# Decoding 4-bit weights by column halves, and projecting the scan's input at the end of the first stage

## The chip, the cores and the metric

The kernel runs on one core of a Trainium2 chip. The metric is device time in microseconds (us) of that core for one execution, and a kernel's time is the median of its runs.

## The reference

Four layers of a gated model, each x = x + tanh(g) * attention-like part, then x = x + tanh(g) * feed-forward part, on x of 4 x 256 x 256 (T = 1024 rows of D = 256). The change touches the code of three of these parts: the first attention, the first feed-forward part (its weights are 4-bit codes with a scale for every 32 inputs) and the state-space scan of the fourth layer, whose input is the context and not x, so that the kernel computes it beside the first feed-forward part.

```python
# layer 0, feed-forward: 4-bit weights
idx = jnp.stack([W_packed & 15, W_packed >> 4 & 15], -1).reshape(N, -1)
W = (NVFP4_LUT[idx].reshape(N, K // 32, 32) * scales[:, :, None]).reshape(N, K)   # gate, up: 2048x256; down: 256x2048
# then down(gelu(gate(x)) * up(x)) on the normalized x

# layer 3, scan (hidden_states = context, 4x256x128)
x = jnp.einsum('bld,ed->bel', hidden_states, in_proj_w)      # the scan's side projection, 256 channels
x = silu(conv(x, conv_w, 4 taps) + conv_b)
dt_low, Bm, Cm = jnp.split(jnp.einsum('bdl,ed->bel', x, x_proj_w), [8, 24], axis=1)
dt = softplus(jnp.einsum('brl,dr->bdl', dt_low, dt_proj_w) + dt_proj_b)
# 256 steps: state = state * exp(dt * A) + dt * u * B ; y = sum(state * C)
```

## The kernel before

The kernel is a row of eight stages, `stage0` to `stage7`. Each is a block in which SyncE (SP, which issues most DMAs), TensorE (PE), VectorE (DVE), ScalarE (ACT) and GpSimd (POOL) run their own instruction lists, tied by semaphores; the next block begins when all five have ended. Memory is three large regions (regA, regB, regC) cut by hand, and some tiles of their own.

`stage0` is the first attention. SP loads x, projections, context and constants, and then the packed weights of the next stage: `load_packed` (line 205) issues for gate, up and down one DMA of codes (1 MB) and eight of scales (128 KB each, one row of scales spread over 16 partitions, line 207). PE projects the context to queries and keys (line 281), makes the energies (286), turns h and the attention matrix (185) and makes the mixing product (299). ACT takes the exponentials. DVE normalizes x (168), takes four maxima (311), divides, copies the turned attention, adds the result to x (330), and in between decodes weights: `dequant_on_vector` (216, 218, 226) is two tensor_scalars and one scalar_tensor_tensor over 128x2048, each waiting for the one before. A weight matrix takes two such steps (`par` 0 and 1). Four run in `stage0`: gate 0 after the maxima, gate 1 after the copies, up 0 and up 1 at the very end.

`stage1` holds the first feed-forward part and most of the scan. It first loads six constants of the scan (417). PE waits for them, projects the context in two halves of channels into the same pair of PSUM banks (`project_context`, 506), the second after ACT has copied the first to `xpad` (452), and turns h (185). DVE normalizes x, then convolves (`convolve`, 588 and 591); ACT takes Silu (458), PE makes `project_bc` (514). Then comes a loop over 32 units u: column chunk u mod 16 of the 2048 hidden columns, for one half of the rows. In each unit PE runs `gate_up(u+1)` (542) and `down(u)` (555), ACT the gelu (465), DVE the gated product `gated(u+1)` (674), and DVE has one more job: the two steps of the down weights in units 0 and 1, splitting rows in 2 and 3, nothing in unit 4, `softplus` in units 5 to 8 (620, 626, 631, 632, with ACT's squares, 447, between), and from unit 9 on one scan group for most units (654, 659, 667), which needs a row that PE spreads over the partitions (498). `down` of the first two units waits for its weights.

ACT takes units in pairs: gelu(0), gelu(1), then other work such as exponentials, then gelu(2), gelu(3). Each change of function set costs it a table load. DVE takes all in the order written.

## Time and profile before

| | us |
|---|---|
| runs (three) | 868.91, 872.73, 874.93 |
| median | 872.73 |
| the profiled execution | 877.0 |
| its span, first to last instruction | 875.2 |
| stage 0, from the start of the span | 0 to 48.9 |
| stage 1 | 48.9 to 267 |
| stages 2 to 7 | 267 to 875.2 |

The profiled execution is a single one and 0.5% above the median. Times in rows are from the start of its span. A row of the timeline is one instruction or several alike in a row (x4: four records); one PE matmul of 32-bit numbers shows as two records. "Idle before" is how long the engine had nothing to run, and what ended that. The granted clock is 1.00 for TensorE's full 2.4 GHz and 0.50 for 1.2 GHz. A DMA's time to landing counts from its issue on SP.

### The profile page before, as it was taken

The page shows a single profiled execution, that of the slowest core. Times are in us where ns is not written, and L with a number is a line of the kernel's source. Part 1 is how long each engine was busy: PE and PEld are TensorE (multiplying, and loading weights), DVE is VectorE, ACT ScalarE, POOL GpSimd, SP SyncE. Part 2 cuts the span into 40 slices and gives each one's busy share as a digit, 9 for nine tenths or more (in the row PEclk, how much of TensorE's full clock was granted, in tenths as well). Part 3 has the DMA queues.
Part 4 walks back from the last instruction along what each step waited for, and adds up shares of the span by engine and source line. Part 5 has one row for each costly group of instructions (what it writes and reads, how often), then busy time and mean ns, then how long its engine had stood idle before and what let it go on. Part 6 is the DMA issues. An engine that isn't in the chain of part 4 may idle for free. (4 is left out here: it accounts for less than half of the span.)

```text
span 875.2 us, 9489 instructions
## 1 busy us (share of the span) xinstructions
PE 649.1 (74%) x2849; PEld 403.9 (46%) x2849; DVE 647.2 (74%) x1331; ACT 355.6 (41%) x607; POOL 179.2 (20%) x184
## 2 busy tenths in 40 slices
PE   4549979999994547499928798889881687338991
PEld 3324545545553436367816455455450133235650
DVE  5988568997978887796546879889848988652344
ACT  5023476545421522455325455665622444402220
POOL 0000001211210000377261010110110255006651
PEclk9759999999996865699969779999986555558996
DMA  8500002454458406146420123433632500102225
GB/s 243 126 14 0 7 0 49 82 86 70 80 91 222 134 0 214 42 125 137 103 83 0 49 70 76 97 74 70 140 54 47 141 25 1 44 5 84 91 79 169
DMA packets 58151, 70.56 MB, mean 81 GB/s; under 512 B 16043, under 2 KB 41523, under 8 KB 56950
## 3 DMA queue, kind: packets, MB, share of 16 engines
q1 hardware_dynamic: 44934, 40.97, 16.7%
q0 software_dynamic: 13168, 28.97, 16.3%
q8 instruction: 25, 0.41, 0.2%
q14 instruction: 24, 0.20, 0.1%
HBM read 42.79 MB, written 10.36 MB: 61 GB/s over the span
## 5 line engine op out<-in xcount | busy, mean ns | idle before, releaser
L542 PE MATMUL ps<-hT,regA 128*128 128x512 f32 x256 | 116.7, 599 | 0.8 <-ACT hT L455 0.8
L1964 PE MATMUL ps<-regA,regD 128*34 128x256 f32 x256 | 71.5, 404 | 12.5 <-DVE h L2090 9.6
L542 PEld LDWEIGHTS ps<-hT,regA 128*128 128x128 f32 x256 | 48.9, 192 | 53.3 <-issue 48.9
L555 PE MATMUL ps<-regA,regC 128*128 128x256 f32 x256 | 64.5, 397 | 9.8 <-DVE regC L674 7.2
L555 PEld LDWEIGHTS ps<-regA,regC 128*128 128x128 f32 x256 | 47.7, 194 | 35.3 <-DVE regC L674 22.0
L719 POOL DMA_DIRECT2D yssm<-regB x19 | 23.0, 1212 | 185.2 <-DVE regB L667 185.2
L465 ACT ACTIVATE regC<-ps 128x512 f32<-128x512 f32 x32 | 19.0, 597 | 84.1 <-PE ps L542 83.9
L1811 ACT ACTIVATE regA<-ps 128x512 f32<-128x512 f32 x64 | 38.1, 596 | 31.6 <-PE ps L1950 31.0
L2070 DVE TENSOR_REDUCE regC<-ps 128x4 f32<-128x960 f32 x64 | 40.1, 685 | 9.6 <-PE ps L1914 9.6
L659 DVE TENSOR_TENSOR_SCAN regB<-regB 128x512 f32<-128x512 f32 x38 | 44.5, 1213 | 2.8
L1764 POOL DMA_DIRECT2D yssm<-regC x13 | 15.6, 1202 | 135.7 <-DVE regC L2111 119.1
L1309 POOL DMA_INDIRECT regA<-h_rows,regA x31 | 33.1, 1067 | 40.2 <-DVE regA L1586 31.1
L1964 PEld LDWEIGHTS ps<-regA,regD 128*34 128x34 f32 x256 | 24.3, 115 | 36.6 <-issue 10.3
L674 DVE TENSOR_TENSOR regC<-regC,ps 128x512 f32<-128x512 f32 x32 | 21.9, 683 | 24.1 <-ACT regC L465 23.6
L1622 DVE TENSOR_TENSOR regB<-regB,ps 128x176 f32<-128x176 f32 x23 | 7.8, 338 | 39.8 <-ACT regB L1368 39.8
L185 PE MATMUL ps<-ident,h 128*128 128x128 f32 x112 | 20.6, 353 | 22.3 <-DVE h L168 20.8
L173 ACT ACT_TABLE_LOAD x7 | 9.0, 1283 | 63.6 <-PEq L245 26.8
L1445 PE MATMUL ps<-regB,regA 128*128 x124 | 33.9, 397 | 0.0
L1903 PE MATMUL ps<-ident,regA 128*128 128x128 f32 x192 | 28.4, 311 | 6.5 <-DVE regA L2061 3.6
L1309 POOL DMA_INDIRECT regB<-h_rows,regB x23 | 22.5, 979 | 49.1 <-DVE regB L1581 42.4
L1445 PE MATMUL ps<-regA,regB 128*128 x92 | 32.2, 474 | 0.0
L2223 POOL TENSOR_TENSOR regB<-regB 128x1024 f32<-128x1024 f32 x8 | 21.7, 2710 | 47.4 <-DVE regB L2382 47.4
(419 smaller groups left out, 1572.8 us busy)
## 6 DMA issues: line engine op xcount, KB each, us to landing
yssm<-regB POOLq DMA_DIRECT2D x19, 512.0 KB, 5.0
regC<-bc_rows SPq DMA_DIRECT2D x26, 256.0 KB, 3.8
yssm<-regC POOLq DMA_DIRECT2D x13, 512.0 KB, 6.8
regB<-in_L_w SPq DMA_DIRECT2D x4, 1088.0 KB, 11.8
y_rows<-regA SPq DMA_DIRECT2D x31, 128.0 KB, 2.6
regB<-in_L_w SPq DMA_DIRECT2D x1, 2176.0 KB, 13.0
regC<-in_L_W SPq DMA_DIRECT2D x2, 1024.0 KB, 10.5
h_rows<-h SPq DMA_DIRECT2D x4, 512.0 KB, 6.7
```

What stands on the lines that cost most here:

```text
L542: m = nc.tensor.matmul(ps[:, 2 + 2 * (u % 2) + j, :], w[:, k * 2048 + c * P:k * 2048 + (c + 1) * P], hT[:, k, hf * HALF:(hf + 1) * HALF], ...
L555: m = nc.tensor.matmul(ps[:, t // 2, (t % 2) * D:(t % 2 + 1) * D], itm[:, u % 2, t * P:(t + 1) * P], WDv[:, c // 2, c % 2, :], start=(c == ...
L659: v.mark(nc.vector.tensor_tensor_scan(hs[:, k, :], dA[:, g % RD, k].rearrange("p b l -> p (b l)"), dBu[:, k, :], 0.0, ALU.mult, ALU.add))
L674: nc.vector.tensor_tensor(itm[:, u % 2, :], gel[:, u % 2, :], ps[:, 3 + 2 * (u % 2), :], ALU.mult).then_inc(s_itm, 1)
L719: nc.gpsimd.dma_start(y, hc[:, g % 2], accum_op=ALU.add).then_inc(s_y, 16)
L1309: nc.gpsimd.indirect_dma_start(xg[:, i % NG, :], None, h_rows, bass.IndirectOffsetOnAxis(rowid[:, i:i + 1], 0)).then_inc(s_got[i % NG], 16)
L1445: m = nc.tensor.matmul(ps[:, block_banks(u)[1], 0:GU], lhs, W[:, bass.ds(at + k * GU, GU)], start=k == 0, stop=k == KD - 1)
L1811: nc.scalar.activation(prob[:, n % 4, :], ps[:, 4 + n % 2, :], ACT.Exp, scale=SCALE4).then_inc(s_p, 1)
L1903: m = nc.tensor.transpose(ps[:, blk // 2, c0:c0 + P], flat(src[:, b % 2, t])[:, blk * P:(blk + 1) * P], ident[:, :])
L1964: m = nc.tensor.matmul(ps[0:VW, 6 + j % 2, (n % 2) * S:(n % 2 + 1) * S], vaug[:, 2 * b + kt, hd, :], prob[:, n % 4, kt * S:(kt + 1) * S], ...
L2070: nc.vector.tensor_reduce(dst[:, :, :, j], sc[:, :, :, lo:hi], AX.X, ALU.max, negate=True).then_inc(s_mx, 1)
L2223: nc.gpsimd.tensor_tensor(w, w, mx_wide(am2[:, t % 2], 1, FF // BLK), ALU.subtract).then_inc(s_rs, 1)
```

## The change

The packed weights of gate and up are loaded and decoded by halves of 1024 columns. All scan constants are now allocated outside the stages, so that `stage0` can write them.

- Loads: in `stage0` SP issues five sets of nine DMAs in place of three: gate first half, up first half, down (whole), gate second half, up second half; then the six scan constants, which `stage1` no longer loads. The second halves lie in tiles that later stages use (`W1q`, `W2q`, `dt_late`, `du_late`).
- `stage0`, DVE: four half steps: gate 0 ahead of the maxima, gate 1 after them, up 0 and up 1 after the copies; none at the end.
- `stage0`, PE and ACT: after the mixing product PE waits for the constants and projects the context into four PSUM banks, ACT copies both halves to `xpad`.
- `stage1`, ACT: Silu stands behind gelu(0); PE runs `gate_up(1)` ahead of `project_bc`.
- `stage1`, DVE: the second halves of gate are decoded in unit 4, those of up in units 5 and 6 inside `softplus`. PE's `gate_up(8)`, the first that reads second halves, waits for them.

```diff
+        def dequant_first(v, code, i, par):
+            dequant_on_vector(v, code, raw_first[i], scl_first[i], par, (WG, WU)[i][:, par * 2048:par * 2048 + CH])
+        def dequant_second(v, code, i, par):
+            dequant_on_vector(v, code, raw_second[i], scl_second[i], par,
+                              (WG, WU)[i][:, par * 2048 + CH:(par + 1) * 2048])
...
+            pieces("gate", raw_first[0], scl_first[0], 0, CH, s_gate1)
+            pieces("up", raw_first[1], scl_first[1], 0, CH, s_up1)
+            pieces("down", raw_down, scl_down, 0, 2 * CH, s_down_pk)
+            pieces("gate", raw_second[0], scl_second[0], CH, CH, s_second)
+            pieces("up", raw_second[1], scl_second[1], CH, CH, s_second)
...
@@ stage0, sync @@
-                    load_packed(sp, s_pk)
+                    load_packed(sp)
+                    for dst, nm in ((in_w, "m_in"), (cw, "m_cw"), (alog, "m_alog"), (xp_w, "m_xp"),
+                                    (dt_w[3 * NBC:3 * NBC + DTR, :], "m_dtw"), (self_[0:3 * NBC, :], "m_sel")):
+                        sp.dma_start(dst, a[nm]).then_inc(s_w, 16)
...
@@ stage0, scalar @@
+                    for k in range(KD):
+                        act.wait_ge(s_xi, k + 1)
+                        c = ps[:, 6 - 2 * k:8 - 2 * k, :].rearrange("p h (b l) -> p (h b) l", b=B // 2)
+                        nc.scalar.copy(xpad[:, k, :, TAPS - 1:LP], c).then_inc(s_xc, 1)
...
@@ stage0, tensor @@
+                    pe.wait_ge(s_w, 96)
+                    for k in range(KD):
+                        for hf in range(2):
+                            m = nc.tensor.matmul(ps[:, 6 - 2 * k + hf, :], in_w[:, k * P:(k + 1) * P],
+                                                 ctxT[:, hf * HALF:(hf + 1) * HALF], start=True, stop=True)
+                        m.then_inc(s_xi, 1)
...
@@ stage0, vector @@
                     norm_on_vector(dve, v, s_var, s_sd, s_h)
+                    dve.wait_ge(s_gate1, 16 * 9)
+                    dequant_first(v, dq, 0, 0)
                     for b in range(B):
...
-                    dequant_on_vector(dve, v, dq, s_pk, range(0, 1))
+                    dequant_first(v, dq, 0, 1)
...
-                    dequant_on_vector(dve, v, dq, s_pk, range(1, 2))
+                    dve.wait_ge(s_up1, 16 * 9)
+                    dequant_first(v, dq, 1, 0)
+                    dequant_first(v, dq, 1, 1)
...
-                    dequant_on_vector(dve, v, dq, s_pk, range(2, 4))
...
@@ stage1, scalar @@
-                    for k in range(KD):
-                        act.wait_ge(s_xi, k + 1)
-                        nc.scalar.copy(xpad[:, k, :, TAPS - 1:LP], pair.rearrange("p (b l) -> p b l", b=B)).then_inc(s_xc, 1)
...
-                    for k in range(KD):
-                        act.wait_ge(s_u, k + 1)
-                        nc.scalar.activation(u_ssm[:, k, :], u_ssm[:, k, :], ACT.Silu).then_inc(s_z, 1)
...
+                            for k in range(KD if w == 0 else 0):
+                                act.wait_ge(s_u, k + 1)
+                                nc.scalar.activation(u_ssm[:, k, :], u_ssm[:, k, :], ACT.Silu).then_inc(s_z, 1)
...
@@ stage1, tensor @@
-                    pe.wait_ge(s_w, 96)
-                    project_context(0)
-                    project_context(1)
...
+                        if u == CH // P:
+                            pe.wait_ge(s_down_w, 3)
...
                     gate_up(0)
+                    gate_up(1)
                     project_bc()
                     for u in range(NU):
-                        if u + 1 < NU:
+                        if 1 <= u < NU - 1:
                             gate_up(u + 1)
...
@@ stage1, vector @@
+                            if k == 0:
+                                dequant_second(v, code[:, 0:CH], 1, 0)
...
+                            if k == 0:
+                                dequant_second(v, code[:, 0:CH], 1, 1)
+                                dve.sem_inc(s_down_w, 1)
...
+                        elif u == SP - 1:
+                            dve.wait_ge(s_second, 16 * 18)
+                            for par in range(2):
+                                dequant_second(v, code[:, 0:CH], 0, par)
```

## Rows read from the trace of the kernel before

**Rows 1.** The page's section 1: busy us, share, instructions of each engine.
```profile
PE 649.1 (74%) x2849; PEld 403.9 (46%) x2849; DVE 647.2 (74%) x1331; ACT 355.6 (41%) x607; POOL 179.2 (20%) x184
```

**Rows 2.** Windows: us, each engine's busy us, granted clock, DMA share, GB/s.
```profile
48.90:71.00 22.10, 15.43 (x37) 7.11 (x38) 15.97 (x37) 10.75 (x13) 0.23 (x5) 0.68 0.06 13
...
94.40:113.40 19.00, 18.33 (x50) 8.76 (x48) 6.32 (x8) 12.10 (x13) 0.00 (x0) 1.00 0.01 2
...
113.40:137.20 23.80, 19.58 (x50) 11.05 (x51) 16.58 (x18) 15.87 (x18) 0.00 (x0) 0.86 0.00 0
...
137.20:256.50 119.30, 115.27 (x358) 62.50 (x356) 105.86 (x136) 59.71 (x76) 22.18 (x19) 1.00 0.46 80
```

**Rows 3.** Timeline of stage 0: start, us, engine, line, operation; [idle before, releaser].
```profile
15.64 0.69 DVE L311 TENSOR_REDUCE regC<-ps 128x2 f32<-128x512 f32 x1 [2.73 <-PE ps L286]
...
18.84 1.22 DVE L216 TENSOR_SCALAR regC<-regB 128x2048 int32<-128x2048 int32 x1
...
21.35 2.29 DVE L226 SCALAR_TENSOR_TENSOR regA<-regC,regB 128x2048 f32<-128x2048 f16 x1
...
28.20 7.45 PE L299 MATMUL ps<-regC,hT 128*128 128x256 f32 x32
...
46.12 2.29 DVE L226 SCALAR_TENSOR_TENSOR regA<-regC,regB 128x2048 f32<-128x2048 f16 x1
```

**Rows 4.** Lines 205 and 207: DMA issues, their starts, landings: codes, two gate scales, all scales.
```profile
L205 SPq DMA_DIRECT2D regB<-in_L_gate_pk x1: 432/432/432, 4.3 to 4.3; - x1
...
DMA to landing us min/median/max: 8.4/12.4/16.5
...
L207 SPq DMA_DIRECT2D regB<-in_L_gate_sc x2: 466/490/513, 7.9 to 8.4; - x2
...
DMA to landing us min/median/max: 9.6/9.9/10.2
...
L207 SPq DMA_DIRECT2D regB<-in_L_down_sc x8: 419/420/430, 13.6 to 16.9; - x8
...
DMA to landing us min/median/max: 8.8/13.4/18.3
```

**Rows 5.** Timeline of the opening of stage 1.
```profile
53.05 2.86 DVE L168 TENSOR_SCALAR h<-x,lnmv,lnsd 128x256 f32<-128x256 f32 x8
...
53.40 3.78 PE L506 MATMUL ps<-ctxT,regB 128*128 128x512 f32 x4 [17.76 <-DMA regB<-in_m_sel]
...
57.22 1.01 ACT L452 COPY regB<-ps 128x1024 f32<-128x1024 f32 x1 [4.44 <-PE ps L506]
...
58.34 0.81 DVE L588 TENSOR_SCALAR regC<-regB,regC 128x1024 f32<-128x1024 f32 x1 [2.41 <-ACT regB L452]
...
59.19 3.92 DVE L591 SCALAR_TENSOR_TENSOR regC<-regB,regC 128x1024 f32<-128x1024 f32 x3
...
65.13 3.70 PE L542 MATMUL ps<-hT,regA 128*128 128x512 f32 x8 [0.82 <-ACT hT L455]
...
69.04 1.28 ACT L465 ACT_TABLE_LOAD   x1
...
70.97 0.69 DVE L674 TENSOR_TENSOR regC<-regC,ps 128x512 f32<-128x512 f32 x1 [3.03 <-ACT regC L465]
...
76.58 1.97 PE L555 MATMUL ps<-regA,regC 128*128 128x256 f32 x8 [0.39 <-DVEq L681]
```

**Rows 6.** Timeline of units 4 to 9 of stage 1.
```profile
100.97 0.69 DVE L674 TENSOR_TENSOR regC<-regC,ps 128x512 f32<-128x512 f32 x1 [6.55 <-ACT regC L465]
...
105.59 1.23 DVE L626 SCALAR_TENSOR_TENSOR regB<-regB,regC 128x1024 f32<-128x1024 f32 x1 [2.33 <-ACT regB L447]
...
118.79 0.69 DVE L674 TENSOR_TENSOR regC<-regC,ps 128x512 f32<-128x512 f32 x1 [0.22 <-DVE regC L632]
...
128.47 3.78 PE L555 MATMUL ps<-regA,regC 128*128 128x256 f32 x8 [3.51 <-DVE regC L674]
...
137.19 1.28 DVE L654 TENSOR_TENSOR regB<-regC,ps 128x512 f32<-128x512 f32 x2 [2.44 <-PE ps L498]
```

More of the change, by code:

```diff
@@ L37, with __init__ @@
 class Steps:
-    def __init__(self, eng, sem):
-        self.eng, self.sem, self.n = eng, sem, 0
+    def __init__(self, eng, sem, done=0):
+        self.eng, self.sem, self.n = eng, sem, done
     def mark(self, ins):
@@ L196, in build @@
         WG, WU, WD = (regA[:, i * 4096:(i + 1) * 4096] for i in range(3))
-        raw = [regB[:, i * 2048:(i + 1) * 2048].bitcast(I32) for i in (0, 1, 3)]
-        scl = [regB[:, i * 2048:(i + 1) * 2048] for i in (2, 5, 4)]
-        s_pk = [sem(f"packed_{nm}") for nm in ("gate", "up", "down")]
+        CH = 1024
+        at_first = (2080, 3104, 4128, 10960)
+        raw_first = [regB[:, o:o + CH].bitcast(I32) for o in at_first[0:2]]
+        scl_first = [regB[:, o:o + CH] for o in at_first[2:4]]
@@ L200, in build, with load_packed, pieces @@
+        raw_second = [w[:, :, :].rearrange("p k n -> p (k n)").bitcast(I32) for w in (W1q, W2q)]
+        scl_second = [w[:, :, :].rearrange("p k n -> p (k n)") for w in (dt_late, du_late)]
+        raw_down, scl_down = regB[:, 6144:8192].bitcast(I32), regB[:, 8192:10240]
+        s_gate1, s_up1, s_down_pk, s_second = (sem("packed_" + nm) for nm in ("gate1", "up1", "down", "second"))
+        s_steps01, steps0 = sem("s01_v"), []
         WDv = WD.rearrange("p (c a n) -> p c a n", c=NHC // 2, a=2)
-        def load_packed(sp, s_pk):
-            for i, nm in enumerate(("gate", "up", "down")):
-                sp.dma_start(raw[i], a[f"L0_{nm}_pk"]).then_inc(s_pk[i], 16)
+        def load_packed(sp):
+            def pieces(nm, raw, scl, c0, n, sm):
+                sp.dma_start(raw, a[f"L0_{nm}_pk"][:, c0:c0 + n]).then_inc(sm, 16)
@@ new lines, in load_packed, with dequant_on_vector @@
+            pieces("gate", raw_first[0], scl_first[0], 0, CH, s_gate1)
[3 more added lines that the diff above has]
+            pieces("up", raw_second[1], scl_second[1], CH, CH, s_second)
+        def dequant_on_vector(v, code, raw, scl, par, o):
+            v.link(nc.vector.tensor_scalar(code, raw, 28 - 4 * par, 19, ALU.logical_shift_left, ALU.arith_shift_right))
+            v.link(nc.vector.tensor_scalar(code, code, 0x8E00, None, ALU.bitwise_and))
+            q = code.bitcast(FP16).rearrange("p (n two) -> p n two", two=2)[:, :, 0]
+            if len(o.shape) == 3:
+                q, scl = (w.rearrange("p (c n) -> p c n", n=D) for w in (q, scl))
+            v.link(nc.vector.scalar_tensor_tensor(o, q, FP16_TO_E2M1, scl, ALU.mult, ALU.mult))
@@ new lines, in build @@
+        cw = arS.take([KD, TAPS + 3])
+        alog = arS.take([KD, NST])
+        bc_rows = nc.dram_tensor("bc_rows", (NBC, T), F32).ap()
+        LATE_AT = [[(0, 1, 2), (3, 5, 7), (9, 13, 15)]] * 3 + [[(3 * i, 3 * i + 1, 3 * i + 2) for i in range(4)]]
+        LATE = [tuple(16 * b + i for i in at) for b, heads in enumerate(LATE_AT) for at in heads]
+        NLATE = len(LATE)
+        bcs = arS.take([T], BF16)
+        selb = arS.take([NBC], BF16)
+        L = (0.810930216216, -0.288527111915, 0.132609761683, -0.0676876229793, 0.0366112232653, -0.0205713852149,
+             0.0118477560374, -0.0067441046525, 0.00401169096238, -0.00325434358357, 0.00198669635839)
@@ new lines, in build @@
+        LDEG = len(L) - 1
+        upper = [z for z in np.roots(L[::-1]) if z.imag > 0]
+        assert len(upper) == LDEG // 2
+        QUADS = [(float(-upper[i].real - 0.5), float(upper[i].imag ** 2)) for i in (3, 2, 0, 1, 4)]
+        NQ = len(QUADS)
+        ar1 = Arena(regC[:, arS.regs[0][1]:])
+        gel = ar1.take([2, HALF])
+        itm = ar1.take([2, HALF])
+        HB = B // 2
+        RD = 6
+        arB, arP = Arena(regB, ar1.regs[0][0][:, ar1.regs[0][1]:]), Arena(regB)
+        dA = arB.take([RD, KD, HB, S])
@@ new lines, in build @@
+        dBu, hs = arB.take([KD, HALF]), arB.take([KD, HALF])
+        hc = arB.take([2, KD, HALF])
+        LP = S + TAPS - 1
+        xpad = arP.take([KD, B, LP])
+        sA, sB = arP.take([T]), arP.take([T])
+        arQ = Arena(regB[:, 3 * 2048:5 * 2048])
+        zpos, sqr = arQ.take([KD, T]), arQ.take([2, T])
+        in_w = arB.take([KD * P])
+        xp_w = arB.take([KD, 3 * NBC + DTR])
+        dt_w = arB.take([D])
+        dtl = arB.take([T])
+        bc1, bc2 = arB.take([T], BF16), arB.take([T], BF16)
@@ L231, in stage0 @@
+        self_ = arB.take([NBC])
+        bc32, bcf = arB.take([T]), arB.take([T])
+        code = arB.take([4 * HALF], I32)
+        sqc = arB.take([NQ])
+        s_w, s_xi, s_xc = (sem("m_" + n) for n in ("w", "xi", "xc"))
         def stage0():
```

93 lines of the change are left out of this document (16 added, 77 removed).

## The prediction

> **What bounds the kernel now.** I read the engines' totals first, then busy time by stretch, then the timeline of the two stages that the diff touches, then the DMA issues. The totals [rows 1] show TensorE (PE) and VectorE (DVE) both busy for three quarters of the span, so neither is the bound everywhere; what counts is which of them ends last in each stretch. The stages stand in series (each begins only when all engines have ended the one before), and everything behind the scan stage is left alone by the change, so I look at 0 to 267 us only.
>
> In stage 0 DVE sets the end. Its last instruction is a decoding step that ends at 46.12 + 2.29 = 48.41 us, while PE has been done since 28.20 + 7.45 = 35.65 us [rows 3]. The next stage begins 0.5 us later, at 48.91.
>
> Stage 1 opens with a serial chain [rows 5]. PE projects the context at half clock (3.78 us for four records), ScalarE (ACT) copies it out (1.01 us), DVE convolves it, ACT takes Silu, and only then can the feed-forward loop turn over: the first gated product starts at 70.97 us, the first down product on PE at 76.58. In the stretch 48.9 to 71 DVE is busy for 16.0 of 22.1 us [rows 2]. From 71 to 94 DVE works nearly without a pause. From 94.4 to 113.4 it has little to do (6.3 of 19.0 us) and waits for PE and ACT. From 113.4 to 137.2 both are partly idle, and PE runs part of it at half clock (granted 0.86 on average). From 137.2 to 256.5 DVE is busy for 105.9 of 119.3 us and PE for 115.3: the scan units follow one another at a fixed pace [rows 2]. What arrives early or late at 137.19, where the first scan group starts, is early or late at the end.
>
> So the sum has three terms: the end of stage 0, the distance from the start of stage 1 to the first down product, and what the decoding steps put into units 4 to 8 cost before the first scan group.
>
> **Price of a decoding step.** A full step is three instructions, from 18.84 to 21.35 + 2.29 = 23.64, with the gap 4.84 us [rows 3]. A half step isn't in the trace. Exact halving gives 2.42 us. Rows of 128x1024 give 0.81 for a tensor_scalar with two pointer operands and 3.92 / 3 = 1.31 for a scalar_tensor_tensor [rows 5], so 0.81 + 0.81 + 1.31 = 2.93 is the upper bound. I take 2.7: the step's tensor_scalars have constants and should be a little cheaper. Before, stage 0 has four full steps (19.4 us). After, it has four half steps (10.8 us); the other four (10.8 us) go to stage 1. DVE's total grows by 2.2 us.
>
> **Term 1, DVE side.** The first half step now stands ahead of the four maxima, where DVE idles for 2.73 us until 15.64, so from 12.91 [rows 3]. It needs the first half of gate's codes and scales. Before, the codes (1 MB) landed at 4.3 + 8.4 = 12.7 and the last scale row at 8.4 + 10.2 = 18.6: eight scale DMAs in 5.9 us, 0.74 each. The last of all landed at 16.9 + 18.3 = 35.2, so a set of nine takes (35.2 - 18.6) / 2 = 8.3 us, of which the codes take 2.4 [rows 4]. With half the bytes: codes at 11.5, scales 0.37 each, all by 14.5. DVE: 14.5 + 2.7 = 17.2, four maxima of 0.69 to 20.0, second half step to 22.7, against 23.7 before. The middle step becomes two halves (5.4 for 4.84), the last two steps are gone: (48.41 - 2 x 4.84) - 1.0 + 0.6 = 38.3 us. The maxima come 1.1 us later, and ACT's exponentials with them, but DVE needs them only at 22.7.
>
> **Term 1, the new tail.** PE now also waits for the six constant loads, runs the eight projection records, and ACT copies twice. The loads are the last of 58 DMAs on SP's queue. Issue isn't the limit: 34 DMAs are issued by 17.3 us, so 58 by about 29. The transfers are: from 10.3 (18.6 - 8.3), one full set of 8.3 and four half sets. A half set takes 4.15 if it halves exactly, 1.2 + 8 x 0.74 = 7.1 if a scale DMA costs the same at half its size. I take 4.3, the end of exact halving plus a little for the doubled count, because the queue was moving data without a pause all that time. That is 10.3 + 8.3 + 17.2 = 35.8, and the constants (some 275 KB, 0.7 us at the codes' rate, plus some latency) land at about 37.3. PE's mixing product, about 1 us earlier than before, ends at about 35. The eight records cost 3.7 at full clock (the row of eight at 65.13) or 2 x 3.78 = 7.6 at half [rows 5]; the first copy hides under the second pair, the second adds 1.1. The stage ends at 37.3 + 3.7 + 1.1 = 42.1 or, wholly at half clock, at 46.0. PE has stood idle for some 2.3 us by then. I take 0.8 for the chance of a fall: 42.9, later than DVE's 38.3. The term is 42.9 - 48.41 = -5.5, between -6.3 and -2.4.
>
> **Term 2, the opening of stage 1.** PE's projection, its wait for the loads and the copies are gone. DVE normalizes for 53.05 + 2.86 - 48.91 = 7.0 us, adds 0.25 for two small instructions, and convolves at once: 2 x (0.81 + 3.92 + gaps) = 9.6. The first gated product starts 16.9 us into the stage, against 70.97 - 48.91 = 22.1 [rows 5]. PE has turned h and can start gate_up(0) at about 8.9; even at half clock it ends by 16. The first full step for the down weights ends at 16.9 + 0.7 + 4.8 = 22.4, where PE's down product starts; before it started at 76.58 - 48.91 = 27.7. ACT has two more table loads (Silu now stands between gelu(0) and gelu(1)) at 1.28 us by the row at 69.04; Silu ends at about 18.6, gelu(1) at 20.5, both ahead of 22.4, so they are hidden. Project_bc ends at 22.3, just in time; a slower PE here would show. I take -5.0, between -5.3 and -3.5.
>
> Of the table loads the Trainium skill says otherwise (ScalarE: Activation LUTs, What ACT_TABLE_LOAD costs): a switch costs its load and a drain, 2.66 us together. In the trace the load at 69.04 follows straight on Silu and gelu starts at 70.33, so no such drain is seen. By the page Silu would end 1.4 us later, project_bc would hold up the down product, and term 2 would be -3.6 in place of -5.0.
>
> **Term 3, units 4 to 8.** The two gate halves (5.4 us) stand before the gated product at 100.97, ahead of which DVE idles for 6.55 us: free, cover 1.1 us to spare. The first up half stands after the maximum at unit 5, where DVE waits 2.33 us for ACT: 2.7 - 2.3 = 0.4 late. The second stands at the end of unit 6, right before the gated product at 118.79 [rows 6]: nothing covers it, so that product starts at about 121.7. Queued behind it is more. gate_up(8) now waits on PE for that step; before it ran from 115.3. PE is idle for nearly 6 us and will resume at 1.2 GHz. But before, PE lost 3.51 us at 128.47 anyway and ran on at half clock (eight records in 3.78 us, against 1.97 at 76.58) [rows 5, 6]; that stall now comes earlier. From 121.7 PE has gate_up(8), down(7), gate_up(9), down(8), gate_up(10): 3 x 3.65 + 2 x 1.95 = 14.9, and some 2.6 lost at half clock: the first scan row at 139.2. DVE was free at 137.19 - 2.44 = 134.75 and is 3 us late: 137.8 (ACT's squares, which it waits for on the way, are paced by DVE and shift with it). Against 137.19 that is +2.0, between +0.6 (DVE's own end) and +3.5 (a longer stretch at half clock). A gain is excluded here: 3 us late is more than the 2.44 us of idle time [rows 6]. In the scan itself nothing changes.
>
> **Sum.** -5.5 - 5.0 + 2.0 = -8.5 us. The profiled execution took 877.0 us (span 875.2 and 1.8 around it), so 868.5 for such a one; it lies 4.3 above the median of the runs, 872.7, and the terms don't depend on that: 864.2 us.
>
> **Rivals.**
> - The stalls are milder: the projection runs at full clock (-6.3) and the first scan group waits for DVE alone (+0.6), with -5.1: -10.8, 861.9 us. For it: DVE's side of both is short. Against it: PE rests before each.
> - The half clock takes more: the projection wholly at half clock (-2.4), gate_up(0) and project_bc late by 1.3 in the opening (-3.8), +3.2 in units 7 to 9: -3.0, 869.7 us. For it: in 48.9 to 71 the granted clock was 0.68, in spite of the projection at 53.4 [rows 2, 5]. Against it: PE's idle time before the projection is now short.
> - Slower: a scale DMA of half the size takes as long as a whole one, 0.74 us. Then a half set takes 7.1, four of them 28.4, the constants land at 48.5, PE (idle for 13 us) needs some 6.2, the copy 1.1: stage 0 ends at 55.8, +7.4, and the total is 7.4 - 5.0 + 2.0 = +4.4, 877.1 us. It decides from where stage 0 ends at 51.4, so from about 0.58 us for a DMA. Against it: the queue moved data without pause, and half the bytes need half the time in it. The Trainium skill speaks for it (DMA: Bandwidth & Descriptors, Rules for kernel authors): gather small transfers into large ones, since under 64 KB it is mostly overhead; the halves are 64 KB. No row here has that size beside this queue.
> - The change does nothing for the time: the 10.8 us of decoding were only moved. Against it: 5.4 of them fall into a measured idle stretch, and the opening is shortened by another cause.
>
> **How the numbers follow.** The forecast has 0.60 (own range 860 to 868), the mild case 0.17, the half-clock case 0.14, the slow transfers 0.06; 0.03 is left for what I don't see. The measurement can tell about 1% (8.7 us) from no change. The forecast lies on that line: half of its chance, all but a little of the mild case's, give faster 0.47; the other half with the half-clock case and most of the slow transfers give same 0.48; slower 0.05. The range of 857 to 872 leaves out the slow transfers and the ends of the others.
>
> **What would show it.** In the profile after: the maxima start at about 17.2, DVE ends stage 0 at about 38.3, the last instruction of stage 0 is ACT's copy at about 42 to 43, PE waits for a DMA before the projection; the first gated product comes 16.9 us into stage 1 and the first down product 22.4; PE idles for about 6 us before gate_up(8) and is granted half clock; the first scan group is 2 us later, counted from the first down product, than before (137.19 - 76.58 = 60.6). I am wrong if the constants land after 40, if DVE's gate halves in unit 4 wait for their loads, or if PE comes late in the opening.

## The result, and the profile after

| | median us | runs | lowest to highest |
|---|---|---|---|
| before | 873.03 | 18 | 864.11 to 878.12 |
| changed | 863.45 | 18 | 854.46 to 869.60 |

The ratio is 0.9884, with a 95% interval of 0.9856 to 0.9913: 1.2% faster; the medians differ by 9.6 us. The ratio is estimated from the runs of the faster state alone, and so is not the quotient of the two medians, 0.9890. The forecast was 864.2, in a range of 857 to 872.

The first profiled execution of the changed kernel has a span of 857.0 us, 18.2 less than before's. That is nearly twice the difference of the medians, so it can't be read alone. Below it is read stage by stage, and then two more profiles of each kernel show which part of it was luck.

Timeline of the changed kernel, end of stage 0 (start, us, engine, line, operation, [idle before, releaser]; line numbers are those of the changed kernel: 224, 225, 229 decode, 389 is a maximum, 410 the update of x, 376 the projection, 344 the copy to xpad, 158 the first instruction of stage 1):

```profile
13.01 0.69 DVE L224 TENSOR_SCALAR regC<-regB 128x1024 int32<-128x1024 int32 x1 [0.16 <-DMA regB<-in_L_gate_sc]
...
14.46 1.23 DVE L229 SCALAR_TENSOR_TENSOR regA<-regC,regB 128x1024 f32<-128x1024 f16 x1
15.72 1.96 DVE L389 TENSOR_REDUCE regC<-ps 128x2 f32<-128x512 f32 x3
...
34.18 2.73 DVE L410 SCALAR_TENSOR_TENSOR x<-ps,tg,x 128x512 f32<-128x512 f32 x4
...
34.23 3.70 PE L376 MATMUL ps<-ctxT,regB 128*128 128x512 f32 x8 [1.39 <-DMA regB<-in_m_sel]
...
37.97 1.01 ACT L344 COPY regB<-ps 128x1024 f32<-128x1024 f32 x1 [0.70 <-PE ps L376]
...
39.28 2.71 DVE L158 BATCH_NORM_STATS2 lnst<-x 128x6 f32<-128x256 f32 x8 [2.38 <-PEq L308]
```

The first half step starts at 13.01 us, in the idle time ahead of the maxima, and the maxima at 15.72. VectorE (DVE) ends at 34.18 + 2.73 = 36.91, and then sits idle for 2.38 us until stage 1 starts. TensorE (PE) waits 1.39 us for the constants, projects in 3.70 us (full clock), and ScalarE's (ACT) second copy ends the stage at 38.98. Before, DVE's decoding ended it at 48.41 [rows 3].

The codes of the first set, and the scale DMAs, the last three of the first set and the last three of the last set (issue, and below it the time to landing):

```profile
L211 SPq DMA_DIRECT2D regB<-in_L_gate_pk x1: 432/432/432, 4.2 to 4.2; - x1
...
DMA to landing us min/median/max: 5.6/5.6/5.6
...
L213 SPq DMA_DIRECT2D regB<-in_L_gate_sc x3: 420/420/421, 7.4 to 8.4; - x3
...
DMA to landing us min/median/max: 4.2/4.4/4.6
...
L213 SPq DMA_DIRECT2D du_late<-in_L_up_sc x3: 420/420/420, 24.2 to 25.1; - x3
...
DMA to landing us min/median/max: 7.1/7.3/8.0
```

The first codes have landed at 4.2 + 5.6 = 9.8 us, the whole first set at 8.4 + 4.6 = 13.0, the last at 25.1 + 8.0 = 33.1; before, the first set was in at 18.6 and the last at 35.2 [rows 4]. Between 13.0 and 33.1 lie five half sets' worth of bytes, 4.0 us each.

Timeline of the opening of stage 1 (556 is gate_up, 606 the convolution, 489 Silu, 694 the gated product, 529 project_bc, 569 down):

```profile
48.31 9.04 PE L556 MATMUL ps<-hT,regA 128*128 128x512 f32 x16 [0.68 <-ACT hT L478]
...
51.87 3.92 DVE L606 SCALAR_TENSOR_TENSOR regC<-regB,regC 128x1024 f32<-128x1024 f32 x3
...
54.57 1.28 ACT L489 ACT_TABLE_LOAD   x1
...
55.72 0.68 DVE L694 TENSOR_TENSOR regC<-regC,ps 128x512 f32<-128x512 f32 x1
...
55.86 2.00 ACT L489 ACTIVATE regC<-regC 128x1024 f32<-128x1024 f32 x2
...
57.92 3.68 PE L529 MATMUL ps<-regC,regB 128*104 128x512 f32 x8 [0.57 <-ACT regC L489]
...
61.44 1.89 PE L569 MATMUL ps<-regA,regC 128*128 128x256 f32 x8
```

The first gated product starts 55.72 - 39.28 = 16.4 us into the stage (before 22.0) and the first down product at 22.2 (before 27.6) [rows 5]. Silu follows its table load at once. The down weights are ready at 61.1 (the third instruction of their decoding step runs from 58.83 for 2.29 us), and the down product starts at 61.44 with no idle time before it: project_bc, which waited for Silu, is the later by some 0.3 us.

Timeline of units 4 to 9, and the start of stage 2:

```profile
85.43 0.69 DVE L694 TENSOR_TENSOR regC<-regC,ps 128x512 f32<-128x512 f32 x1 [1.31 <-ACT regC L485]
...
90.29 1.23 DVE L643 SCALAR_TENSOR_TENSOR regB<-regB,regC 128x1024 f32<-128x1024 f32 x1
...
97.44 0.69 DVE L694 TENSOR_TENSOR regC<-regC,ps 128x512 f32<-128x512 f32 x1 [3.18 <-ACT regC L485]
...
104.87 1.23 DVE L229 SCALAR_TENSOR_TENSOR regA<-regC,du_late 128x1024 f32<-128x1024 f16 x1
...
106.30 5.61 PE L556 MATMUL ps<-hT,regA 128*128 128x512 f32 x8 [6.12 <-DVEq L653]
...
106.32 0.69 DVE L694 TENSOR_TENSOR regC<-regC,ps 128x512 f32<-128x512 f32 x1 [0.22 <-DVE regA L229]
...
122.48 1.28 DVE L674 TENSOR_TENSOR regB<-regC,ps 128x512 f32<-128x512 f32 x2 [0.22 <-PE ps L521]
...
252.41 2.71 DVE L158 BATCH_NORM_STATS2 lnst<-x 128x6 f32<-128x256 f32 x8 [0.32 <-PEq L441]
```

In unit 4 DVE still idles for 1.31 us after two half steps (before 6.55 with none). In unit 5 the half step takes the place of the 2.33 us of waiting for ACT's square: from the gated product to the instruction that had waited it is 4.86 us, before 4.62. The last half step, at the end of unit 6, ends at 106.10. PE has been idle for 6.12 us by then, and gate_up(8) takes 5.61 us in place of 3.60. The first scan group starts at 122.48, which is 61.0 us after the first down product; before it was 60.6 [rows 6]. DVE waits for PE for only 0.22 us ahead of it, in place of 2.44 us before. So on DVE's side the units take 60.8 us in place of 58.2.

### The profile page after: what moved, and what is told of

Read it like the earlier page. It is cut to its first block and busy times, and to the rows that moved or that the text cites. A ratio compares the mean times of both kernels' runs of the same rounds, so it can differ in the third digit from the quotient of the medians.

```text
span 857.0 us, 9521 instructions
## 1 busy us (share of the span) xinstructions
PE 640.4 (75%) x2849; PEld 400.8 (47%) x2849; DVE 648.2 (76%) x1343; ACT 357.0 (42%) x608; POOL 179.2 (21%) x184
## 5 line engine op out<-in xcount | busy, mean ns | idle before, releaser
L556 PE MATMUL ps<-hT,regA 128*128 128x512 f32 x256 | 119.1, 610 | 6.8 <-DVEq L653 6.1
L569 PE MATMUL ps<-regA,regC 128*128 128x256 f32 x256 | 62.5, 388 | 5.0 <-DVE regC L694 3.2
L569 PEld LDWEIGHTS ps<-regA,regC 128*128 128x128 f32 x256 | 46.7, 190 | 29.5 <-DVE regC L694 16.9
L185 PE MATMUL ps<-ident,h 128*128 128x128 f32 x112 | 22.8, 380 | 28.3 <-DVE h L168 26.9
L185 PEld LDWEIGHTS ps<-ident,h 128*128 128x128 f32 x112 | 19.5, 199 | 32.2 <-DVE h L168 29.9
```

What stands on the lines that cost most here:

```text
L185: last = nc.tensor.transpose(o, src[:, t, k * P:(k + 1) * P], (idn or ident)[:, :])
L556: m = nc.tensor.matmul(ps[:, 2 + 2 * (u % 2) + j, :], w[:, k * 2048 + c * P:k * 2048 + (c + 1) * P], hT[:, k, hf * HALF:(hf + 1) * HALF], ...
L569: m = nc.tensor.matmul(ps[:, t // 2, (t % 2) * D:(t % 2 + 1) * D], itm[:, u % 2, t * P:(t + 1) * P], WDv[:, c // 2, c % 2, :], start=(c == ...
```

## Experiments

One table for all profiles, each number a difference of two starts in the timeline: of DVE's first instruction in stage 1, of the first down product, of the first scan group, of DVE's first instruction in stage 2; the last column is the span left from there.

| kernel | stage 1 begins | to first down | to first scan group | to stage 2 | stage 2 begins | stages 2 to 7 |
|---|---|---|---|---|---|---|
| before | 48.95 | 27.63 | 60.61 | 129.95 | 267.14 | 608.1 |
| before, second | 49.00 | 28.86 | 58.06 | 129.95 | 265.87 | 602.5 |
| before, third | 48.98 | 28.42 | 58.07 | 129.91 | 265.38 | 599.2 |
| changed | 39.28 | 22.16 | 61.04 | 129.93 | 252.41 | 604.6 |
| changed, second | 43.53 | 22.07 | 62.25 | 129.94 | 257.79 | 610.1 |
| changed, third | 41.29 | 22.69 | 61.13 | 129.91 | 255.02 | 605.5 |
| e1: all decoding in stage 0 | 48.93 | 22.08 | 60.24 | 129.94 | 261.19 | 608.5 |
| e2: projection in stage 1 | 37.94 | 22.91 | 60.40 | 129.94 | 251.19 | 611.1 |
| e3: last half step in unit 5 | 45.09 | 22.06 | 60.25 | 129.95 | 257.35 | 609.4 |
| e4: constants loaded earlier | 38.02 | 22.07 | 62.07 | 129.94 | 252.10 | 609.1 |
| e5: e3 and e4 | 37.68 | 22.04 | 60.25 | 129.91 | 249.88 | 607.3 |
| e6: e2, constants loaded in stage 1 | 38.67 | 27.42 | 61.61 | 129.94 | 257.64 | 606.4 |
| e7: e2 and e3 | 38.44 | 22.92 | 58.61 | 129.92 | 249.89 | 610.0 |
| e8: e2, Silu ahead of gelu(0) | 37.88 | 26.30 | 62.45 | 129.94 | 256.57 | 605.1 |

The scan itself takes 129.9 us in all fourteen. Stages 2 to 7, whose code is the same in all, take between 599 and 611: a single span says nothing of a difference of 10 us. The first three columns are where the kernels differ.

Times, each median with its ratio to the kernel before on the same chip and the interval (these ratios are not quotients of medians either): changed again 863.81 (0.9889, 0.9852 to 0.9926) and 863.92 (0.9863, 0.9804 to 0.9922); e1 871.10 (0.9932, 0.9895 to 0.9969); e2 863.16 (0.9838, 0.9789 to 0.9887); e3 864.70 (0.9848, 0.9757 to 0.9939); e4 862.94 (0.9860, 0.9793 to 0.9926); e5 856.35 (0.9781, 0.9722 to 0.9841); e6 864.14 (0.9863, 0.9783 to 0.9943); e7 859.94 (0.9801, 0.9731 to 0.9872); e8 864.75 (0.9878, 0.9801 to 0.9955). The intervals of e2 to e8 overlap, so these verdicts rest on the marks in the table; the medians carry only the large steps. Most kernels here have one profile, and the spread between profiles of one kernel, below, is the measure of what a single mark can say.

**The two kernels again, unaltered.**

> The changed kernel once more, unaltered, for a second profile and more times. In the two profiles at hand stage 0 is 9.7 us shorter, stage 1 5.0 us shorter (14.7 together) and stages 2 to 7 3.5 us shorter, although their code is the same; the medians differ by 9.6 us only. Theory (the gain of stages 0 and 1 is fixed at about 14 to 15 us, and single executions of stages 2 to 7 scatter by some us): stage 2 begins at 252 to 253 us again, the ratio to before is 0.983 to 0.992. Rival (part of the gain is an accident of that one execution: the clock granted to TensorE at the projection or in units 7 to 9): stage 2 begins at 255 to 258 us.

> The kernel before once more, unaltered, for a second profile. Theory: stage 1 begins at 48.9 and stage 2 at 266 to 268 us as in the first profile. Rival: the first profile of before was a late one, and stage 2 begins at 262 to 264 us here.

Stage 2 began at 257.8, so the theory of a fixed gain fell and the rival held: part of the first profile was an accident. Timeline of the second profile of the changed kernel:

```profile
36.78 5.40 PE L376 MATMUL ps<-ctxT,regB 128*128 128x512 f32 x8 [2.03 <-DMA regB<-in_m_sel]
...
42.22 1.01 ACT L344 COPY regB<-ps 128x1024 f32<-128x1024 f32 x1 [1.93 <-PE ps L376]
...
43.53 2.71 DVE L158 BATCH_NORM_STATS2 lnst<-x 128x6 f32<-128x256 f32 x8 [5.00 <-PEq L308]
...
65.60 1.96 PE L569 MATMUL ps<-regA,regC 128*128 128x256 f32 x8 [0.70 <-DVEq L702]
...
110.57 6.70 PE L556 MATMUL ps<-hT,regA 128*128 128x512 f32 x8 [6.12 <-DVEq L653]
...
127.85 1.28 DVE L674 TENSOR_TENSOR regB<-regC,ps 128x512 f32<-128x512 f32 x2 [1.30 <-PE ps L521]
```

The constants came 2.6 us later (36.78) than in the first profile, PE ran the projection partly at half clock (5.40 us in place of 3.70: the granted clock is 1.00 until about 38.2 us, in the middle of the records, and then 0.50), and stage 0 ended at 43.2. In units 7 to 9 gate_up(8) took 6.70 us and the scan waited for PE for 1.30 us.

Before scatters too: its opening took 28.9 us and its units 58.1, against 27.6 and 60.6. Stage 2 began at 265.87, just under the 266 to 268 that I expected. The units differ by PE's clock. In the first profile PE ran on at half clock after its wait of 3.51 us [rows 6]. In the second profile of before it ran at full clock after the same wait:

```profile
129.74 1.99 PE L555 MATMUL ps<-regA,regC 128*128 128x256 f32 x8 [3.51 <-DVE regC L674]
```

There the first scan group followed without a wait for PE. So the 60.6 from which I forecast contains 2.4 us of waiting that the other two profiles of before don't have. The opening differs by when the constants land: the projection starts at 53.40, 54.79 and 54.23.

> The changed kernel, unaltered, a third profile and times on the same chip as the version with both edits. Theory: stage 1 begins between 39 and 45 us, by when the constants land (34 to 38) and whether TensorE projects at full or half clock; the first down product 22.1 later, the first scan group 61 to 62.3 after that; stage 2 begins at 252 to 259. Rival (the two profiles of it are both accidents, and the gain in stage 0 is the same each time): 39.2 or 43.5 again with the projection at full clock.

> The kernel before, a third profile. Theory: stage 1 begins at 49.0, first down product 27.6 to 28.9 later, first scan group 58 to 60.6 after that, stage 2 begins at 265.5 to 267.5; stages 2 to 7 take 602 to 611 us, as in all profiles of all kernels so far.

The third profile of the changed kernel lies between:

```profile
36.23 3.70 PE L376 MATMUL ps<-ctxT,regB 128*128 128x512 f32 x8 [3.43 <-DMA regB<-in_m_sel]
```

The third profile of before began stage 2 at 265.38 and left 599.2 us for the rest, both just below what I expected (265.5 to 267.5, and 602 to 611).

Over the three profiles the changed kernel begins stage 2 at 255.1, before at 266.1: 11.1 us earlier, of which the medians show 9.6 (the interval of the ratio, taken on 873, reaches from 7.6 to 12.6).

**e1: the second halves decoded in stage 0.** This undoes the part of the change that moves decoding.

```diff
# stage0, vector, after the update of x
+                    dve.wait_ge(s_second, 16 * 18)
+                    for i in range(2):
+                        for par in range(2):
+                            dequant_second(v, dq, i, par)
# stage1: the four dequant_second and gate_up(8)'s wait removed
```

> From the changed kernel: the four second half steps are moved back to the end of stage 0 (after x is updated), stage 1 has none, and gate_up(8) has no wait for them. Everything else as changed. Theory: VectorE ends stage 0 at 36.9 + 4 x 2.7 = 47.7 us (the loads landed at 34), so stage 1 begins at 48.0 in place of 39.2 (+8.8); the opening stays at 22.2 us to the first down product; from there to the first scan group 60.6 to 61.0 us, as in both profiles, since the delay in units 4 to 8 cost 0.4 us. Sum +8.4 us on the changed kernel, so about 1 us faster to 6 us faster than before (0.994). Rival (the second half steps cost about 2 to 3 us in stage 1): first scan group 58.5 us after the first down product, sum +6 us.

Stage 1 began at 48.93, the opening took 22.1 and the units 60.2; the median was 7.3 us above the changed kernel's on the same chip, the two ratios (0.9932 and 0.9889) are only 3.8 us apart, and stage 2 began 6.1 us later than in the mean of the changed kernel's three profiles. So the moved decoding (10.8 us) is worth some 4 to 7 us: stage 0 gets shorter by 7.6 us (41.4 in the mean of the three profiles, against 48.9), and some of that is lost again in the units. The 60.2 lies near the 60.6 to 61.0 of the theory, as if the half steps cost nothing there, but it contains a wait for PE of 2.42 us:

```profile
131.25 1.29 DVE L671 TENSOR_TENSOR regB<-regC,ps 128x512 f32<-128x512 f32 x2 [2.42 <-PE ps L525]
```

Without it DVE's own work takes 57.8 us, against 60.8 in the changed kernel: the rival, 2 to 3 us in the units, held for DVE's side. The run also shows that the opening's gain has nothing to do with the decoding: 22.1 us here too.

**e2: the projection back in stage 1**, with the constants still loaded in stage 0. PE's projection and ACT's copies stand at the start of stage 1, as in the kernel before.

```diff
# stage1, tensor
+                    pe.wait_ge(s_w, 96)
+                    for k in range(KD):
+                        if k >= 1:
+                            pe.wait_ge(s_xc, k)
+                        for hf in range(2):
+                            m = nc.tensor.matmul(ps[:, 6 + hf, :], in_w[:, k * P:(k + 1) * P],
+                                                 ctxT[:, hf * HALF:(hf + 1) * HALF], start=True, stop=True)
+                        m.then_inc(s_xi, 1)
# stage1, scalar, behind norm_on_scalar
+                    for k in range(KD):
+                        act.wait_ge(s_xi, k + 1)
+                        nc.scalar.copy(xpad[:, k, :, TAPS - 1:LP], pair.rearrange("p (b l) -> p b l", b=B)).then_inc(s_xc, 1)
# stage0: the projection and the two copies removed
```

> From the changed kernel: the projection of the context and its two copies are moved back to the start of stage 1 (the constants are still loaded in stage 0). Theory: stage 0 ends with VectorE at 36.9, stage 1 begins at 37.4 (-1.8). TensorE then projects at half clock (2 x 3.8 us with ScalarE's copy between) before it turns h, so gate_up(0) starts about 13 us into the stage in place of 9; VectorE's convolutions are hardly later (first copy at 5 us, second at 10, both before it needs them), so the first gated product comes at 17 to 20 us, and TensorE's first down product at 25 to 26 in place of 22.2. Sum +1.5 to +2.5 us on the changed kernel. Rival (the projection was the cause of the whole gain in the opening, 5.4 us): first down product at 27.7, sum +3.7. Second rival (only the early loads mattered): first down product at 22.5, sum -1.5.

Timeline of its opening:

```profile
37.94 3.75 PE L542 MATMUL ps<-ctxT,regB 128*128 128x512 f32 x4 [4.38 <-PEq L308]
...
42.79 3.78 PE L542 MATMUL ps<-ctxT,regB 128*128 128x512 f32 x4 [1.10 <-ACT regB L468]
...
46.61 1.02 ACT L468 COPY regB<-ps 128x1024 f32<-128x1024 f32 x1 [3.87 <-PE ps L542]
...
46.37 2.08 PE L185 MATMUL ps<-ident,h 128*128 128x128 f32 x16
...
49.69 0.81 DVE L604 TENSOR_SCALAR regC<-regB,regC 128x1024 f32<-128x1024 f32 x1
...
60.85 1.89 PE L570 MATMUL ps<-regA,regC 128*128 128x256 f32 x8
```

Stage 1 began at 37.94. (Lines: 542 projection, 468 copy, 604 convolution, 185 turning h, 570 down.) Though PE projected at half clock (3.75 and 3.78 us), the second copy was done at 47.6, before DVE asked for it at 49.69, and the first down product came 22.9 us into the stage, 0.6 later than in the mean with the projection in stage 0 and far from the 25 to 26 that I expected: PE was at work from 37.94 on and turned h at full clock (2.08 us for sixteen records, the fourth line). The number is that of the second rival, but the run doesn't show its reason, that only the early loads mattered, since e2 keeps the new order of Silu and gelu too; e6 and e8 part the two. The move of the projection, by which the change is named, gives 0.6 us in the opening (22.3 in the mean of the three profiles) and costs at the end of stage 0: stage 1 begins at 41.4 in their mean, and at 37.9 to 38.7 in the four kernels without the projection there (e2, e6, e7, e8). By the marks the kernel without it is 2.5 us or so faster; by the medians of one chip, 863.16 to 863.81, the difference is inside the noise.

**e6 and e8: what shortened the opening.** Both start from e2.

```diff
# e6: from the end of stage0's queue to the start of stage1's
+                    for dst, nm in ((in_w, "m_in"), (cw, "m_cw"), (alog, "m_alog"), (xp_w, "m_xp"),
+                                    (dt_w[3 * NBC:3 * NBC + DTR, :], "m_dtw"), (self_[0:3 * NBC, :], "m_sel")):
+                        sp.dma_start(dst, a[nm]).then_inc(s_w, 16)
# e8: Silu ahead of the loop on ScalarE, project_bc ahead of gate_up(1) on TensorE (lines moved, none changed)
```

> From the kernel with the projection in stage 1: the six constant loads are moved back to the start of stage 1 too. So of the change the halves and the order gelu(0), gate_up(1), Silu remain. Theory (of the 4.7 us that the opening of stage 1 is shorter there than before, some 2 to 3 come from the loads having landed, the rest from the order): stage 1 begins at 37.9; TensorE projects from 4.5 us into the stage, the second copy ends at 14.2, the convolutions at 19; first down product at 24.5 to 25.5 us into the stage, against 22.9 with loads in stage 0 and 27.7 to 28.9 before. Rival (the order does nothing): 27.7 or later. Second rival (the loads do nothing): 23.

> From the kernel with the projection in stage 1 and the constants loaded in stage 0: Silu stands ahead of gelu(0) again and project_bc ahead of gate_up(1), as before the change. Theory: VectorE's convolutions end at 16.4 us into the stage, Silu at 17.6, the table load and gelu(0) at 19.5, so the first gated product starts at 19.5 in place of 16.5 and the first down product at 25.2 in place of 22.9: +2.3 us. Rival (the order does nothing): 22.9.

e6's projection started only when the loads had landed, 4.6 us into the stage:

```profile
43.30 2.93 PE L542 MATMUL ps<-ctxT,regB 128*128 128x512 f32 x3 [8.78 <-DMA regB<-in_m_sel]
```

and its first down product came at 27.4. That is near the rival by which the order does nothing (27.7). I had expected 24.5 to 25.5, since I followed DVE's convolutions; PE's own list (projection, turning h, gate_up(0) from 54.87) was later than they were. In e8 DVE waited 3.03 us for gelu:

```profile
57.42 0.69 DVE L694 TENSOR_TENSOR regC<-regC,ps 128x512 f32<-128x512 f32 x1 [3.03 <-ACT regC L481]
```

which is 57.42 - 37.88 = 19.5, as expected, and the down product came at 26.3, as project_bc waited for Silu and then ran partly at half clock (5.38 us for eight records, with a mean granted clock of 0.68). At full clock (3.68 us) the down weights, ready at 62.8, would have been the later, and the down product would have come at about 25 (an estimate), as expected. Together with before (mean of three 28.3) this makes a square of four:

| first down product, us into stage 1 | Silu ahead of gelu(0) | Silu behind gelu(0) |
|---|---|---|
| constants loaded in stage 1 | 28.3 | 27.4 |
| constants loaded in stage 0 | 26.3 | 22.9 |

Each of the two alone gives 0.9 or 2.0 us, both together 5.4. What takes the time after one is mended is the other. The square rests on single profiles in three of its fields. The 0.9 is less than the spread of before (27.6 to 28.9), and with 25 in place of 26.3 the order alone would give some 3 us. That both together give most is shown; how the gain divides between them is not.

**e3: the last half step a unit earlier.**

```diff
# softplus
                             dve.sem_inc(s_sqd, 1)
+                        if part == 0 and k == 0:
+                            dequant_second(v, code[:, 0:CH], 1, 1)
+                            dve.sem_inc(s_down_w, 1)
# the same three lines removed from part 1
```

> From the changed kernel: the last half step (up, second halves, par 1) stands at the end of unit 5's softplus part, ahead of the gated product that VectorE waits 3.18 us for ScalarE to release, in place of the end of unit 6. Theory: the step (2.7 us) vanishes in that wait, gate_up(8) no longer waits for VectorE, the product of unit 7 starts some 2.7 us earlier; from the first down product to the first scan group 58 to 60.6 us, as in the two profiles of before (60.6 and 58.1), in place of 61.0 and 62.2: a gain of 2 us (0.2%) on the changed kernel. Rival (the stall only moves, and what it costs is the half clock of TensorE somewhere in units 7 to 9): 61 to 62 us, no gain.

Timeline of e3, units 6 and 7 (the last half step on line 229, the gated products on 694, gate_up(8) on 556):

```profile
101.69 1.23 DVE L229 SCALAR_TENSOR_TENSOR regA<-regC,du_late 128x1024 f32<-128x1024 f16 x1
...
103.27 0.69 DVE L694 TENSOR_TENSOR regC<-regC,ps 128x512 f32<-128x512 f32 x1 [0.35 <-ACT regC L485]
...
105.84 3.60 PE L556 MATMUL ps<-hT,regA 128*128 128x512 f32 x8
...
109.31 0.69 DVE L694 TENSOR_TENSOR regC<-regC,ps 128x512 f32<-128x512 f32 x1 [0.22 <-DVE regC L652]
```

The lines are the last half step's third instruction, the products of units 6 and 7, and gate_up(8) between them. DVE's wait for ACT shrank from 3.18 to 0.35 us, gate_up(8) started at once behind down(6), 3.60 us at full clock, and the product of unit 7 came 6.0 us after that of unit 6, in place of 8.9 (97.44 to 106.32). The units took 60.25, at the upper end of what was expected. One profile with a scatter of 2 us proves little, but all together do: with the last half step in unit 6 seven profiles have 60.4 to 62.5 (mean 61.6), with it in unit 5 three have 58.6 to 60.3 (mean 59.7), with none four have 58.1 to 60.6 (mean 59.2). So the four half steps of stage 1 (10.7 us of DVE's time) cost 2.3 us as the change places them and 0.5 us with the last one in unit 5.

Most of the scatter in these numbers is the wait for PE ahead of the first scan group (0 to 2.44 us). With that wait taken off, the two placements part cleanly: DVE's own time from the first down product on is 60.4 to 61.8 us in the seven profiles with the last half step in unit 6, and 57.6 to 58.2 in the seven others, whether the half steps stand earlier or are absent. The difference of the means is 2.8 us, one half step. The other three half steps cost DVE's end no more than 0.1 us.

**e4: the constants loaded after the second set.**

```diff
             pieces("up", raw_first[1], scl_first[1], 0, CH, s_up1)
+            for dst, nm in ((in_w, "m_in"), (cw, "m_cw"), (alog, "m_alog"), (xp_w, "m_xp"),
+                            (dt_w[3 * NBC:3 * NBC + DTR, :], "m_dtw"), (self_[0:3 * NBC, :], "m_sel")):
+                sp.dma_start(dst, a[nm]).then_inc(s_w, 16)
             pieces("down", raw_down, scl_down, 0, 2 * CH, s_down_pk)
# the same three lines removed from the end of stage0's queue
```

> From the changed kernel: the six constant loads are issued after the second set (up, first half), ahead of the down weights, in place of the end of the queue. Theory: they land before 25 us, TensorE projects straight behind the mixing product (at about 33 to 35), at full clock, 3.7 us, and stage 0 ends with ScalarE's second copy 4.8 us after the mixing product or with VectorE at 37 to 38.5: stage 1 begins at 38 to 40 in every execution, against 39.2 and 43.5 in the two profiles of the changed kernel. Gain on the median of the changed kernel about 2 to 3 us. Rival (the half clock comes anyhow): stage 1 begins at 41 to 43.

> From the changed kernel: both edits together, the constants loaded after the second set and the last half step of up at the end of unit 5's softplus part. Theory (the terms add): stage 1 begins at 38.0, first down product 22.1 later, first scan group 58.5 to 60.3 after that, stage 2 another 129.9 later, at 249 to 250.5; the kernel is 3 to 5 us faster than the changed one and 0.980 to 0.984 of before. Rival (one of the two gains is lost in the other's place): stage 2 begins at 252 to 253.

> From the changed kernel: the projection is back at the start of stage 1 (constants loaded at the end of stage 0's queue), and the last half step of up stands at the end of unit 5's softplus part. Theory: stage 1 begins at 37.9, first down product 22.9 later, first scan group 58.5 to 60.3 after that, stage 2 at 249.5 to 251. Rival (the shorter middle was an accident of the other profile): stage 2 at 252.5.

In e4 and e5 PE projected without a wait, straight behind the mixing product. Timeline of e5 (projection, second copy, stage 2):

```profile
32.73 3.60 PE L376 MATMUL ps<-ctxT,regB 128*128 128x512 f32 x8
...
36.36 1.01 ACT L344 COPY regB<-ps 128x1024 f32<-128x1024 f32 x1 [0.70 <-PE ps L376]
...
249.88 2.71 DVE L158 BATCH_NORM_STATS2 lnst<-x 128x6 f32<-128x256 f32 x8 [0.32 <-PEq L441]
```

Stage 1 began at 38.02 and 37.68. e5 began stage 2 at 249.9, where the sum of the terms had it, and e7 as well. e5's median was 856.35 when the changed kernel's was 863.92 on the same chip, 7.6 us less, where 3 to 5 were expected and the marks give 5.2. It is 2.2% below before (interval 1.6 to 2.8), and the ranges of its runs and the changed kernel's hardly overlap (850.41 to 862.78 and 855.35 to 866.35). e4 alone was not timed beside the changed kernel on one chip.

## Why the prediction was right, and where it was not

The time was right (864.2 for 863.45), and the ratio, 0.9884, lies just beyond the 1% that parts "faster" from "no change", which had been given nearly equal chances; its interval (0.9856 to 0.9913) reaches over that line. That the number came within 1 us is partly luck: terms 1 and 2 were larger than forecast, and the profiles have 11.1 us by the start of stage 2 where the forecast had 8.5. The working, step by step, against the three profiles of each kernel:

- **Price of a half step.** 2.7 was forecast; 13.01 to 15.69 is 2.68.
- **Term 1, -5.5; measured -9.7 in the first profile, -7.6 in the mean of three (e3, with the same stage 0, was later: 45.09, the mean of four is -6.7).** The mechanism was right: DVE is no longer last; the constants, the projection and the copy are. The constants were forecast to land at 37.3, the stage to end at 42.9; the landings were 34.2, 36.8 and 36.2 (37.5 and 37.6 in e3 and e1), the ends 39.0, 43.2 and 41.0. Mis-sized was the first set: its codes landed at 9.8, not 11.5, and its scales at 13.0, not 14.5, so the maxima began at 15.7 and not at 17.2. My bound of -6.3 for the best case was therefore too tight: the first and the third profile lie beyond it.
- **The slow transfers** (a scale DMA costs the same at half its size) didn't come: a half set took 4.0 us in the first profile and 4.5 in the two others, near the half of 8.3 and far from 7.1. The first profile's 4.0 us less 1.2 for the codes leaves 0.35 us for each scale DMA of 64 KB, against 0.74 for 128 KB. The Trainium skill (DMA: Bandwidth & Descriptors, Rules for kernel authors) advises against many small transfers, since one under 64 KB is mostly overhead. Here, where many of 64 KB are queued behind one another, half the bytes took about half the time; the trace decides.
- **Term 2, -5.0; measured -5.5 in the first profile, -6.0 in the mean.** The first gated product (16.4 for 16.9), the end of project_bc (22.3) and the first down product (22.2 for 22.4, 22.3 in the mean) came where they were forecast; the mean is larger because before's other two profiles open later. The size was right, by a wrong division. I named the absent projection first, and followed DVE; e2 shows that the projection could have stayed (22.9), and the square of e6 and e8 that the loads and the order of Silu and gelu carry it, most of it together. I had put the order down as a cost (two more table loads, hidden) and not as a gain.
- The sentence on the drain: by the Trainium skill (ScalarE: Activation LUTs, What ACT_TABLE_LOAD costs) a table switch costs 2.66 us. In the trace Silu starts at 54.57 + 1.29 = 55.86, behind the load at once, and project_bc wasn't late. The trace and the page differ, and the trace decides.
- **Term 3, +2.0; measured +0.4 in the first profile, +2.6 in the mean.** Most steps were right: the gate halves free with 1.31 us to spare (1.1 forecast), 6.12 us of idle time for PE (nearly 6), half clock on gate_up(8) (5.61, 6.70 and 6.06 us for 3.60), and DVE 2.6 us late by its own work (3 forecast). Too large was PE's delay behind it: the scan was forecast to wait 1.4 us for PE, and waited 0.22, 1.30 and 0.68. And the sum stood on a profile of before that had itself waited 2.44 us for PE; against that one profile the mean is +0.9, against before's mean +2.6. That the forecast of +2.0 lies between is in part chance.
- **The mild and the half-clock rival** were not wholly other cases: single executions do what either has. The projection ran at full clock in the first and third profile and partly at half clock in the second, while gate_up(8) was slowed in all three. Against before's first profile, stage 2 began 14.7, 9.4 and 12.1 us earlier (the mild rival had 10.8, the half-clock rival 3.0); no profile came near 3.0.
- **That the change does nothing** fell with e1: the moved decoding is worth 7.3 us by the medians, 3.8 by the ratios and 6.1 by the marks.

What stays open: why the same queue of DMAs delivers the constants at 34.2 in one execution and 37.6 in another, and why stages 2 to 7 scatter by 12 us. No run here was made to tell. The three profiles of before show that it goes with PE's clock: these stages took 608.1, 602.5 and 599.2 us at a mean granted clock of 0.78, 0.80 and 0.81, PE was busy for 427, 414 and 409 us, and DVE for 440 in all three. It isn't all, since two profiles of the changed kernel at 0.79 are 5.5 us apart.

## What to carry to other kernels

When work is moved to fill an engine's idle time, look at what the move hangs behind: here the projection went to the end of a stage and with it the stage's end went to the last DMA of a queue, and in e2 and e4, where it was left alone or six small loads were issued earlier, stage 2 began 3 to 4 us earlier, by one profile each. Place a step of 2.7 us where its engine waits for another one, not where another one waits for it: one unit earlier the same step gave 1.9 us back, and 2.8 of DVE's own time. And compare marks inside the profile (stage begins, first product) over several profiles: the spans scatter by more than the change.

## What the runs showed of the hardware that I had not expected

- PE's clock after a short rest is not to be told from the rest's length. Before the projection PE rested for 2.03 us and then ran eight records in 5.40 us. The granted clock was 1.00 through the rest and the first 1.4 us of the records, and fell to 0.50 only then, while PE was at work. In another execution of the same kernel it rested for 3.43 us and ran them in 3.70 (granted 1.00). After 1.39 us it took 3.70, after 3.99 and 4.37 (e1, e3) 6.55 and 6.22. In the kernel before, the same rest of 3.51 us was followed by eight records in 3.78 us in one execution and in 1.99 in two others.
- Halving the size of the first DMAs of a queue brought them in by more than half their transfer: the codes needed 5.6 us from issue to landing in place of 8.4 [rows 4], 2.8 us less, where half the bytes at 2.4 us for 1 MB would give 1.2. In the other two profiles of each kernel it was 5.5 and 5.6 in place of 7.8 and 7.7.
